# Rows sorted to experts per pair of batches, the gathers moved, and indirect DMAs without waits between them

## The reference, cut to what matters

```
h = _layernorm(x, axis=-1) * (1 + cb) + sb
x = x + gb * _L0_ffn_ref(h, ...)

def _L0_ffn_ref(x, router_w, expert_w1, expert_b1, expert_w2, expert_b2):
    router_probs = softmax(einsum('bnc,ec->bne', x, router_w))
    expert_weights, expert_idx = top_k(router_probs, 2)
    expert_weights = expert_weights / (expert_weights.sum(axis=-1, keepdims=True) + 1e-09)
    h = gelu(einsum('bnc,efc->bnef', x, expert_w1) + expert_b1, approximate=False)
    out_all = einsum('bnef,ecf->bnec', h, expert_w2) + expert_b2
    out_k = take_along_axis(out_all, expert_idx[..., None], axis=2)
    return (out_k * expert_weights[..., None]).sum(axis=2)
```

## Time and profile before

| | us |
|---|---|
| median of three runs | 1514.68 |
| lowest and highest | 1509.36, 1516.99 |
| the profiled execution | 1507.7 |
| its span, first to last instruction | 1506.0 |
| TensorE busy in it | 1243.9 (83%) |
| VectorE busy | 981.3 (65%) |
| ScalarE busy | 914.2 (61%) |
| GpSimd busy | 529.1 (35%) |

### The profile page before, as it was taken

One profiled execution on the slowest core, in us unless ns is written; L12 is line 12 of the kernel. 1 busy time (PEld: TensorE's weight loads), 2 busy tenths in 40 slices (PEclk: granted clock), 3 DMA queues, 4 the chain that ended last, 5 costly groups with the idle time before them and its releaser, 6 DMA issues. The chain is left out here.

```text
span 1506.0 us, 26566 instructions
## 1 busy us (share of the span) xinstructions
PE 1243.9 (83%) x8185; PEld 778.0 (52%) x8186; DVE 981.3 (65%) x2622; ACT 914.2 (61%) x1319; POOL 529.1 (35%) x588
## 2 busy tenths in 40 slices
PE   6996768988896589999999999989998996665560
PEld 4875668978853123333433343333344874465560
DVE  5563466666678398888888788878887574420222
ACT  4562623423365588988888888878886664233330
POOL 6245745466286411221112111211120024444444
PEclk9998879999988799999999999999999897787885
DMA  9800022322246432222222122222200501112222
GB/s 265 231 1 28 26 63 85 101 77 75 77 153 185 115 48 36 35 35 36 37 37 36 39 36 40 41 40 40 40 8 8 169 15 48 51 32 67 77 60 74
DMA packets 114787, 100.44 MB, mean 67 GB/s; under 512 B 10882, under 2 KB 99424, under 8 KB 114656
## 3 DMA queue, kind: packets, MB, share of 16 engines
q1 hardware_dynamic: 101256, 78.64, 22.0%
q0 software_dynamic: 8192, 16.79, 4.0%
q10 hardware_dynamic: 5208, 3.43, 0.9%
HBM read 54.51 MB, written 44.30 MB: 66 GB/s over the span
## 5 line engine op out<-in xcount | busy, mean ns | idle before, releaser
L2413 ACT ACTIVATE probs<-scores_ps 128x1024 f32<-128x1024 f32 x512 | 507.4, 1027 | 81.8 <-PE scores_ps L2440 77.2
L2440 PE MATMUL scores_ps<-q_pack,k_pack 64*128 64x512 f32 x1024 | 245.4, 492 | 43.0 <-ACT probs L2413 21.2
L2457 PE MATMUL pv_ps<-probs,v_pad 128*32 128x512 f32 x2048 | 274.7, 609 | 0.1
L2440 PEld LDWEIGHTS scores_ps<-q_pack,k_pack 64*128 64x128 f32 x1024 | 96.2, 184 | 315.6 <-issue 170.1
L2340 POOL TENSOR_TENSOR squares<-sparse_scores 128x512 f32<-128x512 f32 x32 | 41.0, 1280 | 472.9 <-DVE sparse_scores L2578 472.9
L1391 ACT ACTIVATE hidden_experts<-pre_experts 128x512 f32<-128x512 f32 x94 | 59.3, 631 | 130.5 <-DVE pre_experts L1325 67.6
L2650 DVE TENSOR_SCALAR_CACHE_REDUCE junk<-sparse_scores,at 128x1024 f32<-128x1024 f32 x96 | 122.8, 1279 | 3.4
L1413 PE MATMUL up_ps_experts<-x_t_experts,up_weights_now_experts 128*128 128x128 f32 x752 | 108.2, 290 | 16.8 <-DVE up_weights_now_experts L1320 6.6
L1413 PEld LDWEIGHTS up_ps_experts<-x_t_experts,up_weights_now_experts 128*128 128x128 f32 x752 | 95.8, 200 | 22.6 <-DVE up_weights_now_experts L1320 16.5
L3210 POOL DMA_INDIRECT expert_rows_dram<-expert_input_tail,send_to_tail x64 | 61.5, 961 | 127.0 <-DVE send_to_tail L3352 108.7
L1420 PE MATMUL down_ps_experts<-weights_t,hidden_experts 128*128 x736 | 99.9, 280 | 0.0
(11 more groups left out here) (406 smaller groups left out, 2414.9 us busy)
## 6 DMA issues: line engine op xcount, KB each, us to landing
q_pack<-q_pieces_dram SPq DMA_DIRECT2D x120, 64.0 KB
k_pack<-k_pieces_dram SPq DMA_DIRECT2D x120, 64.0 KB
expert_rows_dram<-zeros SPq DMA_DIRECT2D x1, 6400.0 KB, 23.2
x_rows_experts<-expert_rows_dram SPq DMA_DIRECT2D x25, 256.0 KB
expert_rows_dram<-y_rows_experts SPq DMA_DIRECT2D x46, 128.0 KB
q_pieces_dram<-q_pieces_prep SPq DMA_DIRECT2D x8, 512.0 KB, 3.6
k_pieces_dram<-k_pieces_prep SPq DMA_DIRECT2D x8, 512.0 KB, 5.7
expert_rows_dram<-zeros SPq DMA_DIRECT2D x1, 2560.0 KB, 18.2
```

What stands on the lines that cost most here:

```text
L2413: act.activation(probs[:, kt % 2, 2 * pair : 2 * pair + 2, c * 512 : c * 512 + 512], scores_ps[n % 2][:].rearrange("p (h t) -> p h t", h=2 ...
L2440: ins = pe.matmul(scores_ps[n % 2][:, head * 512 : head * 512 + 512], k_pack[group % 2][rows, pair, kt * P : kt * P + P].bitcast(F32R), q_ ...
L2457: ins = pe.matmul(pv_ps[32 * j : 32 * j + 32, c, :], v_pad[:, group % 2, kt, j, :], probs[:, kt % 2, j, c * 512 : c * 512 + 512], start=(k ...
```

## The change: what it does

- Rows are sorted to experts per pair of batches. A pair has 4096 rows: 32 full tiles and 7 begun ones, 39, rounded up to 40 so that a pair is 10 rounds. The kernel has 80 tiles in 20 rounds. `positions` adds, for the second batch of a pair, the counts of the first.
- In `experts0` the waits for a tile between indirect DMAs are gone, for sends and for gathers. `rows_here` is raised once per pair, when both batches are sent.
- GpSimd gathers batches 0 and 1 after the first pair's ten rounds, one after the other, and sums each; the power for both comes at the end of its list. Batch 2's gather is no longer in this block.
- VectorE's loop is cut once, at round 16, for the statistics of batch 0; those of batch 1 stand behind the last round.
- In `combine_and_project`, `pick.0` issues all 16 gathers of batch 2 before its own two, and the stages `comb.2` and `stats.2` move in `PREP_ORDER` from the first line to the second, behind `sqout.1`.

```
-BATCH_TILES = (2 * T // P + E - 1, E * CAPACITY // P)
+UNROLL = 4
+PAIRS_OF_BATCHES = B // 2
+ROW_TILES = (-(-(2 * 2 * T // P + E - 1) // UNROLL) * UNROLL, E * CAPACITY // P)
+ROW_PARTS = (PAIRS_OF_BATCHES, B)
...
-        self.trash = B * self.tiles * P
+        self.trash = ROW_PARTS[layer] * self.tiles * P
...
                 def positions(p):
                     pe.wait_ge(sel_ready, nth("be", p))
                     to = take("po", p)
-                    for c in range(2):
-                        for m in range(NT):
-                            pe.matmul(to[:, c * E : c * E + E], g.ones_b[:], sel[:, c * NT + m, :], start=(m == 0), stop=(m == NT - 1))
+                    for m in range(2 * NT):
+                        pe.matmul(to[:, 0:E], g.ones_b[:], sel[:, m, :], start=(m == 0), stop=(m == 2 * NT - 1))
                     for c in range(2):
                         at = 2 * E + c * NT * E
                         pe.matmul(to[:, at : at + NT * E], g.before[:], sel[:, c * NT : c * NT + NT, :].rearrange("p n e -> p (n e)"), start=True, stop=False)
+                        for m in range(c * NT):
+                            pe.matmul(
+                                to[:, at : at + NT * E].rearrange("p (n e) -> p n e", e=E), g.ones_b[:], bc(sel[:, m, :], NT), start=False, stop=False
+                            )
...
-    STEPS = B * moe.tiles // UNROLL
-    AHEAD = -(-moe.tiles // UNROLL)
+    STEPS = PAIRS_OF_BATCHES * moe.tiles // UNROLL
+    AHEAD = moe.tiles // UNROLL
     HALF = UNROLL // 2
 
-    STATS_AT = (13, 20)
+    STATS_AT = 16
...
-                tile_at = [0]
-
-                def next_tile():
-                    tile_at[0] += 1
-                    pool.wait_ge(y_ready, tile_at[0] + 2)
-
                 for b in range(B):
                     if b >= SENT_EARLY:
                         moe.scale_and_shift(pool, step, b)
                         step.settle()
-                        moe.send_rows(g, pool, b, apart=next_tile)
+                        moe.send_rows(g, pool, b)
                     pool.wait_ge(g.rows_sent[b], 16 * 2 * NT)
-                    pool.sem_inc(rows_here, moe.tiles)
-                pool.sem_inc(rows_here, max(moe.tiles, 2 * UNROLL))
-                for b in range(B - 1):
-                    pool.wait_ge(y_free, b * (2 * AHEAD) + (2 * AHEAD + 1))
-                    tile_at[0] = max(tile_at[0], (b + 1) * moe.tiles)
-                    gather(pool, g, picked, b, [(k, n) for k in range(2) for n in range(NT)], g.rows_picked, apart=next_tile)
-                    if 1 <= b <= EARLY:
-                        pool.wait_ge(var_ready, b)
-                        g.ln1.invert(pool, b - 1).then_inc(rstd_ready, 1)
+                    if b % 2 == 1:
+                        pool.sem_inc(rows_here, moe.tiles)
+                pool.sem_inc(rows_here, 2 * UNROLL)
+                pool.wait_ge(y_free, 2 * AHEAD + 1)
+                for b in range(EARLY):
+                    gather(pool, g, picked, b, [(k, n) for k in range(2) for n in range(NT)], g.rows_picked)
                     pool.wait_ge(g.rows_picked, (b + 1) * (16 * 2 * NT))
-                    if b < EARLY:
-                        for part in weighted_sum(g, picked, b, NT):
-                            part(pool, step)
-                        pool.sem_inc(summed, 1)
+                    for part in weighted_sum(g, picked, b, NT):
+                        part(pool, step)
+                    pool.sem_inc(summed, 1)
+                for b in range(EARLY):
+                    pool.wait_ge(var_ready, b + 1)
+                    g.ln1.invert(pool, b).then_inc(rstd_ready, 1)
                 pool.wait_ge(rstd_ready, EARLY)
...
+                with dve.Fori(0, STATS_AT) as i:
+                    tiles_of(i, [])
+                parts = stats(0)
+                done = STATS_AT
+                for at in range(0, len(parts), UNROLL):
+                    tiles_of(done, parts[at : at + UNROLL])
+                    done += 1
                 with dve.Fori(done, STEPS) as i:
                     tiles_of(i, [])
+                for part in stats(1):
+                    part()
...
 PREP_ORDER = """
-pick.0 cols center.0 center.1 norm.0 comb.2 pick.1 norm.1 turn.0 pick.2 colk turn.1 stats.2 ht.0 vrow pick.3 ht.1 q.0 rowk sqk.1 p0.0.0 pick.4
-square.0.0 sv.1 skk.1 rest.0.0 pick.5 skc.1 k.0 sqd.1 k.1 p0.0.1 p2.0.0 sqout.1 rstd.2 square.0.1 svk.1 qkout.0.0 q.1 p0.1.1 heads rest.0.1 square.1.1
+pick.0 cols center.0 center.1 norm.0 pick.1 norm.1 turn.0 pick.2 colk turn.1 ht.0 vrow pick.3 ht.1 q.0 rowk sqk.1 p0.0.0 pick.4
+square.0.0 sv.1 skk.1 rest.0.0 pick.5 skc.1 k.0 sqd.1 k.1 p0.0.1 p2.0.0 sqout.1 comb.2 stats.2 rstd.2 square.0.1 svk.1 qkout.0.0 q.1 p0.1.1 heads rest.0.1 square.1.1
...
                 def pick(i):
                     all_parts = [(k, n) for k in range(2) for n in range(NT)]
+                    if i == 0:
+                        gather(pool, g, picked, EARLY, all_parts, g.rows_picked)
                     n = len(all_parts) // PICKS
                     gather(pool, g, picked, B - 1, all_parts[i * n : i * n + n], last_picked)
...
                 def combine(b):
+                    if b == EARLY:
+                        dve.wait_ge(g.rows_picked, (EARLY + 1) * (16 * 2 * NT))
                     if b == B - 1:
                         dve.wait_ge(last_picked, 16 * 2 * NT)
```

More of the change, by code:

```diff
@@ L328, in front @@
         sel = a.sb("selected", [P, 2 * NT, E], BF16)
[L329 to L330 removed]
+        more = a.sb("more", [P, E, 2 * NT])
+        full_tiles = a.sb("full_tiles", [P, 2 * NT])
         earlier = a.sb("earlier", [P, E, E])
[L332 to L336 removed]
+        tiles = a.sb("tiles", [P, E])
+        ahead = a.sb("ahead", [P, E, E])
+        start = a.sb("start", [P, E])
+        start_row = a.sb("start_row", [P, E])
+        first_row = a.sb("first_row", [P, PAIRS_OF_BATCHES, E])
         logits_now = a.sb("logits", [P, TILES, E])
@@ L520, in more_consts @@
                         step(pool.memset(g.expert_rank[:, e : e + 1], float(E - e)))
-                    for n in range(NT):
+                    for n in range(2 * NT):
                         step(pool.memset(full_tiles[:, n : n + 1], float(n * P)))
@@ L526, in more_consts @@
                             step(pool.memset(earlier[:, e, 0:e], 1.0))
-                    for b in range(B):
-                        step(pool.memset(first_row[:, b, :], float(b * moe.slots)))
-                    step(pool.memset(moe.tile_expert[:, B * moe.tiles :], 0))
+                    for p in range(PAIRS_OF_BATCHES):
+                        step(pool.memset(first_row[:, p, :], float(p * moe.slots)))
+                    step(pool.memset(moe.tile_expert[:, PAIRS_OF_BATCHES * moe.tiles :], 0))
                     step(pool.iota(tile_no[:], pattern=[[1, moe.tiles]], base=0, channel_multiplier=0, allow_small_or_imprecise_dtypes=True))
```

54 lines of the change are left out of this document (18 added, 36 removed).

## The result

The changed kernel takes 1560.67 us (median of four runs, 1558.78 to 1561.62), the kernel before 1515.1 beside it: 1.030 times as long (95% interval 1.028 to 1.032), 46 us slower. The forecast was 1552, with a range of 1516 to 1574. The profiled execution took 1558.8 us (span 1557.0), 51.0 us more than the span before.

A forecast was written before the change was run, and what follows sets the result against it. TensorE was taken to bound the experts' block, and GpSimd's gathers to be the projecting block's path. -23.1 + 38.0 + 2.5 + 20.2 + 0.2 = +37.8 us on 1514.7 gave 1552 us, range 1516 to 1574.

The forecast's parts named there:

- Fewer rounds: Experts' block: 20 rounds instead of 23, three rounds at 7.71 us saved on TensorE's path, -23.1 us.
- Bursts: Experts' block: 64 back-to-back DMAs at 0.9 us (bounds 0 and 1.07), 14.4 a burst; 57.6 - 19.6 = +38.0 us.
- the 7.6 that the prediction let stay: Experts' block: surplus us from GpSimd's sums and scalings and small things, taken to remain after the change.
- End of the block: Experts' block's end: batch 1's statistics and power behind the last round, 4.1 us in series, +2.5 net (0 to 4).
- Projecting block: Block after the experts: 16 more gathers at 1.26 us ahead of batch 3's, on the path, +20.2 us (15 to 30).
- only moved: Projecting block: VectorE's sum of batch 2 with its statistics, about 9 us, merely changes place, waiting for its gather.
- the rival at 1562: Projecting block: it stops as well during 28 DMAs in a row, +30 for it, total +47.6; chance 0.12.
- the prediction's own sign: Projecting block: if VectorE waits for batch 3's gather just before its sum, the step is right; for TensorE, the block stopped.
- Front: Before the experts' block: 8 more small matrix products per pair, 0.4 less 0.2 for shorter index steps, +0.2 us.
- Bursts are free: Rival, experts' block: back-to-back DMAs cost TensorE nothing, GpSimd's vector work made the surplus; -19.8, 1495 us; chance 0.13.
- the 19.6 us of surplus: Experts' block of the kernel before: extra time in rounds beside 21 back-to-back DMAs, 0.93 us each.
- mild price of 0.25 a DMA: Rivals from the projecting block's 12 gathers: gathers alone mild, 1532 us, chance 0.19; all 64 mild, 1511, chance 0.06.

The follow-up runs named there:

- e1: Changed kernel with a wait for one more tile behind each of the 64 indirect DMAs of the experts' block; 1.0029 of the kernel before (1368.5 us).
- e3: Changed kernel with waits for a tile behind the 32 gathers of batches 0 and 1 alone; 1.0011 of the kernel before (1368.5 us).
- e4: Kernel before with only the waits between indirect DMAs taken out, 80 DMAs in five bursts; 0.9994 of the kernel before (1368.5 us).
- e6: Changed kernel, batch 2's gathers in the experts' block (batch 0's rows), waits for a tile put back there; 1509.73 us, 1.0017 of the kernel before.
- e5: Changed kernel, batch 2's 16 gathers issued in the experts' block with batch 0's row numbers, no waits; 1565.75 us, 1.0391 of the kernel before.
- e11: Changed kernel with the experts' block's waits back and VectorE's and GpSimd's work reordered in the projecting block; 1519.73 us, 1.0077 of the kernel before.
- second group: Changed kernel rerun, two variants moving batch 2's gathers, and the kernel before, on one chip; changed kernel 1552.53 us, kernel before 1507.79.
- e2: Changed kernel with waits for a tile behind the 32 sends of the experts' block alone; 1.0007 of the kernel before (1368.5 us).
- e7: Changed kernel with 1 to 4 GpSimd memsets behind each indirect DMA, in both mixtures of experts; 1464.6 us (one run), kernel before 1369.92.
- e9: Changed kernel, gathers of batches 0 and 1 as plain 64 KB DMAs from fixed rows; 1373.9 us (one run), kernel before 1369.92.

## Why the prediction was right

The sum said +37.8 us; the medians differ by 45.6 and the traces by 51.0, so against the traces it was 13 us low. The 1560.67 measured lies within the range of 1516 to 1574. The signs and the places were right: the rounds, the four long intervals, the sum of batch 3 some 17 us later. The sizes of two terms were low, and one term had half of its reason wrong. And one thing was luck: the forecast was measured on a chip of the kind that its trace came from, a condition that it didn't name; on the second kind the variants e1 to e3 are +1 to +3 us.

**Fewer rounds, -23.1.** Right. Undisturbed rounds stay at 7.71 us, and there are 20. On the second kind, where nothing else disturbs, rounds 0 to the last take 154.7 us in e1 and 178.6 in e4: -23.9.

**Bursts, +38.0.** The mechanism held on the chip of the forecast, and the size was low. 74.1 us of surplus and 1.0 before round 0 (201.28 to 210.62 is 9.3 us, in the kernel before it was 8.3) against 27.2 make +48. The long intervals hold 16.4 to 20.7 us over 7.71 each (the 2.7 counted with the third), and GpSimd's scaling and sums are in them. Those alone can be read on the second kind: rounds 0 to 19 of e1 take 154.7 us, 8.2 over 19 undisturbed ones, near the 7.6 that the prediction let stay. With the 1.0 before round 0 that leaves 66.9 us for the four bursts, 16.7 each, 1.05 a DMA: over the 0.9 taken, just inside the upper bound of 1.07. The windows of the earlier trace rows, by which 14.4 us seemed right, end with the burst, while the loss goes on: from 224 to 230, behind the last send, TensorE is busy 2.28 of 6 us at a clock of 0.50, its lower level. That the waits removed are the cause is shown by e6 against e5 (-56 us), and by the rounds of e6 and e11: 166.1 us instead of 217.7 in the changed kernel on e6's chip, 51.6 less for four bursts. What is left there over e1's 154.7 are bursts of up to nine that bunch up in spite of the waits (an interval of 12.6 us around five of them in e6).

**End of the block, +2.5.** Measured +6.9, and +7.4 on the second kind (16.5 in e1, 9.1 in e4). The statistics and the power cost 4.5 us, 4.1 were worked out: the last result is there at 436.9, the power over at 441.4. But from there to the next block it is 6.1 us, where it was 3.6 from the last store's issue (410.40, in the kernel before) to 414.03. The row of the drain says what fills them: GpSimd's queue drains for 5.27 us behind its power (441.57 to 446.84), and the next block begins at 447.54. In the kernel before, the drain took 6.58 us, but it ran from 400.2 to 406.8 and was over before the last result was there (410.2). That an engine which ends last brings its own way out of the block with it was no term of the sum.

**Projecting block, +20.2.** Measured +17.2, 19.1 on the second group's chip, and 19.9 (e2 against e4) on the second kind. The size was right, the reason half: 9 to 10 are the gathers, 9 to 10 the stages `comb.2` and `stats.2` that stand later (e5, e6). The prediction called the moved sum "only moved". That the machine might stop in this block (the rival at 1562) happened in part: ScalarE's and VectorE's waits of 25.33 and 6.86 us for TensorE's results. It cost nothing: e1's block is as long (112.3 us) where nothing stops, since GpSimd's and VectorE's lists set its end. By the prediction's own sign (VectorE waits for the gather of batch 3 just before its sum) the path was right only by a hair here, 0.41 us, and clearly in e1, 4.95.

**Front, +0.2.** +1.6 up to GpSimd's scaling of batch 2 in the first traces, -0.2 up to round 0 in those of group 2: within what two executions differ.

**The rivals.** "Bursts are free" is refuted where it was asked and true on the second kind of chip. There -23.9 + 7.4 + 19.9 leaves +3, and the variants e1 to e3 measure +1 to +3: the sum of that rival, -20, was wrong too, since it also credited the 19.6 us of surplus, of which that chip shows little: e4's rounds take 178.6 us, 9.0 over 22 undisturbed ones, and the vector work is in that. The mild price of 0.25 a DMA, 3 us on 12 in the projecting block, had no row either; the kernel before on the first kind and e4 on the second differ there by 0.9 us (92.8 and 91.9). By the Trainium skill (SBUF — State Buffer, "SBUF: two separate sides"), TensorE and ScalarE never wait on anyone and a DMA is not slowed by compute nor the reverse. The second kind agrees (21.55 of 22 us). On the first kind TensorE is busy 5.88 of 14 us, so a burst isn't free there; whether a port of SBUF has to do with it no run here shows.

What stays open is what in the chip holds the results back, what sets the two kinds apart (the chip itself, or a condition that stayed with it as long as a group ran), and on the first, whether the pitch of the DMAs, their indirect form, or the place of each in TensorE's work makes the stop. Pitch and form were tried (e7, e9), on a chip that could not show it.

## What to carry to other kernels

Before a change is judged by one chip, run the kernel before on a second: here 9% lay between two chips, nearly all of it in sections with back-to-back indirect DMAs, and the change costs 46 us on one kind, while its variants cost 1 to 3 on the other. Where GpSimd issues many indirect DMAs beside a loop of TensorE, a wait for the loop's progress behind each is cheap insurance: it costs 0 on one kind and gains some 13 us a burst of 16 on the other (51.6 for four, in the rounds). That does not hold where GpSimd's issuing is itself the path. In a stretch with such a burst, put work that needs only memory next to it, and what needs TensorE's results behind: e11's rows speak for that, no pair of runs tests it. And an engine that comes to end last in a block costs its drain as well.

## What the runs showed of the hardware

Two kinds of chip: the kernel before takes 1368.5 and 1369.9 us on two, 1508 on two others and 1515 in the first measurement. In the attention the traces of both kinds have the same clock (0.99) and the same time, 722.6 to 723.6 us. On the slower kind a burst of indirect DMAs lets TensorE go on for some 7 us, and then its results come late to VectorE and ScalarE. In the rows above they wait 10.6, 13.8 and 25.3 us for them, and the waits end between 2 us before and 5 us after the burst's last DMA is issued; sends and gathers alike. On the other kind TensorE stays busy through bursts at the same pitch of 1.26 us.

GpSimd's queue drains for 5.27 us (6.58 in the kernel before) at the end of the experts' block, the same on both kinds, and the next block waits for it when GpSimd ends last.
